# A nine-stage kernel whose stages meet once instead of twice, without GpSimd's Drain after three of them, and with one pair of down products moved forward

## The reference

```
h = layernorm(x)*(1+ca)+sa;  x = x + ga * L0_attn(h)   # causal softmax attention and a "geo" attention
h = layernorm(x)*(1+cb)+sb;  x = x + gb * L0_ffn(h)    # 32 routed experts of 64, top 4, and a shared expert
...
xe = zeros(E, C, D).at[eid, posc].add(...)             # at most 128 tokens an expert
h  = silu(xe @ W1) * (xe @ W3);  ye = h @ W2
yrows = ye[eid, posc] * gate;    out = sum over the 4 choices + silu(X@sw1.T)*(X@sw3.T)@sw2.T
...
h = layernorm(x)*(1+ca)+sa;  x = x + ga * L1_attn(h)   # short convolutions and a weighted delta rule, chunks of 64
h = layernorm(x)*(1+cb)+sb;  x = x + gb * L1_ffn(h)    # RMS norm, top 2 of 8 experts, hidden 352
```

## Time and profile before

| | us |
|---|---|
| median of 3 runs | 2004.95 |
| lowest and highest | 2000.4, 2006.43 |
| profiled execution, its own time | 2002.02 |
| its span, first to last instruction | 2000.1 |

### The profile page before, as it was taken

The page is one execution under the profiler, slowest core; times in us unless marked ns, Lnnn a source line. Parts: engine busy times, 40 slices in busy tenths (PEclk is TensorE's granted clock), DMA queues, the critical chain, the costliest instruction groups (busy, mean ns, idle before and its releaser), DMA issues. The chain is left out here.

```text
span 2000.1 us, 50931 instructions
## 1 busy us (share of the span) xinstructions
PE 1612.7 (81%) x17727; PEld 1252.1 (63%) x17727; DVE 1473.4 (74%) x4099; ACT 1185.8 (59%) x2762; POOL 1096.3 (55%) x1141
## 2 busy tenths in 40 slices
PE   5599999998788695698847777777789607999994
PEld 4478888887577442344325555555568607999993
DVE  8688888887499542699979999999667624555556
ACT  4566666665279721577828888887366404565551
POOL 3278888887000286233348888888437773444440
PEclk8799999999899798799969999999766658999998
DMA  4000000000501132521000000000401112222216
GB/s 120 18 3 3 4 4 4 4 3 3 219 28 41 42 45 35 147 63 43 11 0 1 1 2 1 1 1 1 185 23 48 52 60 62 66 64 65 64 51 257
DMA packets 84954, 92.34 MB, mean 46 GB/s; under 512 B 11696, under 2 KB 69296, under 8 KB 84000
## 3 DMA queue, kind: packets, MB, share of 16 engines
q1 hardware_dynamic: 67840, 62.66, 9.9%
q0 software_dynamic: 14560, 22.24, 4.3%
q10 hardware_dynamic: 2304, 4.20, 0.5%
HBM read 46.14 MB, written 42.91 MB: 45 GB/s over the span
## 5 line engine op out<-in xcount | busy, mean ns | idle before, releaser
L2275 POOL TENSOR_TENSOR delta_A<-delta_A,delta_sW 128x256 f32<-128x256 f32 x256 | 193.7, 757 | 79.1 <-ACT delta_sW L2122 53.0
L2045 PE MATMUL delta_u<-delta_m,tables_sb 128*128 128x256 f32 x512 | 166.7, 407 | 82.0 <-DVE delta_m L2195 82.0
L694 ACT ACTIVATE attn_p_att<-attn_score,attn_mx 128x32 f32<-128x32 f32 (+7 forms) x512 | 150.4, 409 | 134.7 <-DVE attn_mx L756 134.7
L2895 POOL DMA_INDIRECT choice_rows<-ffn_y,ffn_xg x135 | 129.7, 961 | 170.9 <-DVE ffn_y L3002 167.4
L2122 ACT ACTIVATE delta_sW<-delta_W,tables_sb 128x256 f32<-128x256 f32 x256 | 126.7, 506 | 79.9 <-DVE delta_W L2217 76.1
L2045 PEld LDWEIGHTS delta_u<-delta_m,tables_sb 128*128 128x128 f32 x512 | 87.1, 190 | 132.7 <-DVE delta_m L2195 126.0
L2041 PE MATMUL delta_u<-delta_v_own,tables_sb 128*128 128x256 f32 x512 | 153.8, 383 | 8.7 <-DVE xnT L2182 8.7
L2852 POOL DMA_INDIRECT rows<-mix_rows,mix_slot x128 | 125.5, 980 | 47.9 <-issue 38.6
L1324 POOL DMA_INDIRECT exp_rows<-rows,slot_token x32 | 33.1, 1033 | 190.4 <-SPq L142 180.9
L2217 DVE TENSOR_TENSOR delta_W<-delta_W,delta_u 128x128 f32<-128x128 f32 x512 | 133.1, 280 | 4.5
L2204 DVE TENSOR_TENSOR delta_u<-delta_u,delta_prod 128x256 f32<-128x256 f32 x256 | 109.8, 429 | 17.8 <-PE delta_u L2045 4.2
(11 more groups left out here) (396 smaller groups left out, 4691.4 us busy)
## 6 DMA issues: line engine op xcount, KB each, us to landing
ffn_xg<-rows SPq DMA_DIRECT2D x135, 66.0 KB, 1.8
acc<-route_zero SPq DMA_DIRECT2D x10, 832.0 KB
comb_rows<-choice_rows SPq DMA_DIRECT2D x32, 256.0 KB, 5.3
rows<-route_rows SPq DMA_DIRECT2D x8, 640.0 KB, 3.5
load_rows<-in_x SPq DMA_DIRECT2D x16, 256.0 KB, 3.8
bT<-acc SPq DMA_DIRECT2D x16, 256.0 KB, 4.1
qT<-acc SPq DMA_DIRECT2D x16, 256.0 KB, 4.7
x_kept<-xT SPq DMA_DIRECT2D x16, 256.0 KB, 2.1
```

Of the source, the lines that this page charges most:

```text
L694: last = nc.scalar.activation(p_att[:, gr, PAIR_OFF[n]:PAIR_OFF[n] + SLOT * (n + 1)], S[:, gr, c:c + SLOT * (n + 1)], ACT.Exp, bias=mx[:, ...
L2045: nc.tensor.matmul(corrections(h, pp % 2), g.t("same_head"), m1[:, h].rearrange("p t d b -> p (t d b)"), start=False, stop=True).then_inc( ...
L2275: nc.gpsimd.tensor_tensor(A[:, t % 8], A[:, (t - 1) % 8], sW[:, t % RING], ALU.add).then_inc(k.A, 1)
L2895: nc.gpsimd.indirect_dma_start(g.choice_rows, bass.IndirectOffsetOnAxis(xg[:, n % RING, D:D + 1].bitcast(U32), 0), y[:, n % RING, :], None ...
```

## The change

1. Leaving a scope no longer clears semaphores and no longer holds the second meeting. The scope's semaphores go onto a list, `Scope.retired`.
2. Opening the next scope's block clears what is on the list, on GpSimd, in front of its branch into that stage. Since the next stage takes its semaphores before that, it gets other numbers, and what is cleared one stage later can be two ranges instead of one. At the end of the program the last scope is cleared and one `all_engine_barrier()` is held.
3. The blocks of the experts, the mix and the FFN are closed without GpSimd's Drain. The other engines issue their Drain there, then signal and wait with semaphore instructions.
4. In the experts' round 0 TensorE makes the down products after `shared_down(0)` and in front of `turn(1)` and `shared_up(1)`, and VectorE makes `y` in front of `add_shared(0)`. Rounds 1 to 15 are as before.

```diff
--- before.py
+++ after.py
@@ -123,6 +123,8 @@
 class Scope(ExitStack):
 
 
+    retired = []
+
     def __init__(self, nc, name):
         super().__init__()
         self.nc, self.name, self.taken = nc, name, []
@@ -142,11 +144,12 @@
         super().__exit__(*exc)
         if exc[0] is None:
 
-            self.nc.clear_and_free_semaphores(self.taken)
-            self.nc.all_engine_barrier()
-
-    def block(self):
-        return self.enter_context(self.nc.Block())
+            Scope.retired.append(self.taken)
+
+    def block(self, drain=True):
+        while Scope.retired:
+            self.nc.clear_and_free_semaphores(Scope.retired.pop())
+        return self.enter_context(self.nc.Block(no_gpsimd_drain=not drain))
 
 
 RC = CH // SLOT
@@ -1315,7 +1318,7 @@
         gate_ps, val_ps, shared = s.ps("gate_ps"), s.ps("val_ps"), s.ps("shared")
         c = s.sems("sw_ready w13 w2 turned x_copied up gate hid down y up_s gate_s hid_s shared x_done added0 added1")
         gathered = [s.sems("gathered", n).gathered for n in range(LAST + 1)]
-        block = s.block()
+        block = s.block(drain=False)
         chunk = lambda i: bass.ds(i * CH, CH)
 
         @block.gpsimd
@@ -1386,10 +1389,13 @@
             for i in range(0, LAST + 1):
                 make_up(i)
                 shared_down(i)
+                if i == 0:
+                    make_down(i)
                 if i < LAST:
                     turn(i + 1)
                     shared_up(i + 1)
-                make_down(i)
+                if i > 0:
+                    make_down(i)
 
         @block.scalar
         def _(act):
@@ -1454,8 +1460,11 @@
             shared_hidden(0)
             for i in range(0, LAST + 1):
                 hidden(i)
+                if i == 0:
+                    output(i)
                 add_shared(i)
-                output(i)
+                if i > 0:
+                    output(i)
                 if i < LAST:
                     shared_hidden(i + 1)
 
@@ -3203,6 +3212,9 @@
         mix_phase(nc, dram, g)
         ffn_phase(nc, dram, g)
         combine_phase(nc, dram, g, out)
+        while Scope.retired:
+            nc.clear_and_free_semaphores(Scope.retired.pop())
+        nc.all_engine_barrier()
 
 
 def kernel(**inputs):
```

## The result

| | us |
|---|---|
| median of the changed kernel, 5 runs | 1981.78 |
| lowest and highest | 1979.2, 1984.25 |
| median before, then 5 runs | 2003.12 (2000.4 to 2006.43) |
| ratio to before, 95% interval | 0.9893 (0.9877 to 0.9908) |
| profiled execution, its own time | 1984.25 |

The change takes 21.3 us off.

A forecast was written before the change was run, and what follows sets the result against it. No engine fills any stage, so the time is nine stage lengths plus what lies between them. Meetings 6.0 - 0.1, Drains 9.8 - 0.1 and round 0 1.0 make 16.6 us: 2004.95 to 1988.4, said as 1988, range 1982 to 1996.

The forecast's parts named there:

- Second meetings, 6.0: At eight transitions between stages, the time from first to second release goes, together 6.0 us; the ninth, at the end, stays.
- Three Drains, 9.8: GpSimd's Drains after experts, mix and FFN (5.28, 1.44, 3.08 us) leave the transitions and are hidden in the next stages: 9.8.
- GpSimd now meets them as the Drain in front of the clear: The three Drains do not vanish but move to the next stage's start, covered there; cost 0.1 us at the projection.
- First gather, nothing lost: Experts' first gather is held until VectorE's cast of `w13` ends, so the whole 0.6 us is kept; otherwise 0.4 is lost.
- Round 0, 1.0: Experts' round 0: earlier down products and `y` free GpSimd's first addition; most returns as a wait before the third; gain 1.0 us.
- I take 0.2 for what is not given back: Delay of `turn(1)` and `shared_up(1)` by the early down products, not regained before `make_up(1)`: 0.2 us off 1.2.
- later rounds of `y` have 1.2 us of slack more each: In the experts, each `y` after round 1 has 1.2 us of slack more.
- Rivals 2 to 4: Drain's wait returns as later landings (1998.2, chance 0.05); code fetches exposed at transitions (1997.2, 0.06); fetches queue there (2014.8, 0.04).
- The sum: Whole kernel: 6.0 - 0.1 + 9.8 - 0.1 + 1.0 = 16.6 us gained.
- the median before is 2.9 us above the profiled execution, and the forecast for the median is 2004.95 - 16.6: Base of the whole-kernel forecast: median before 2004.95 us, profiled execution 2002.02; less 16.6 gives 1988.4, said as 1988.

The follow-up runs named there:

- plain Drain behind the release: Changed kernel with one plain GpSimd Drain added in front of each clear, at the start of the next stage; 2040.94 us in one run.
- the first comparison: First measurement of the changed kernel against the kernel before, five runs each: 1981.78 against 2003.12 us, ratio 0.9893.
- series 1: Later measurements of each part alone and the changed kernel again (1982.81 us, ratio 0.9914), beside 17 runs of before (median 2001.76).
- series 3: Later measurements beside 23 runs of before (2049.32 us): changed kernel a third time 2041.15, ratio 0.9943; with round 1 reordered too 2038.15, ratio 0.9944.

## Why the prediction was right and wrong, point by point

- **Second meetings, 6.0: right, perhaps more.** The change alone gives 9.4 (6.0 to 12.6). The stages that have only this term fell, in the means of three traces each, by 1.5 (attention), 0.3 (route) and 1.1 us (delta), where 0.7, 0.7 and 0.9 were forecast.
- **Three Drains, 9.8: the size right, the mechanism wrong.** Alone they give 11.6 (8.2 to 15.2). The step that failed is "GpSimd now meets them as the Drain in front of the clear": that Drain takes 0.1 us. Why the clear's Drain doesn't take the cost over is open. The error cost nothing in the sum, because the place where the prediction put the three Drains was covered anyway, as the plain Drain behind the release shows: the size came right without the mechanism.
- **First gather, nothing lost: right.** 2.33 us long against 2.3 forecast, ending 1.0 after the cast, and it moves with the cast. That a whole gather is left when the cast ends holds for this case (1.0 us) and not for the one that begins with the cast (0.1).
- **Round 0, 1.0: the place right, the size a little high.** The stage's length gives 0.5 to 0.9. The term that was mis-sized is "I take 0.2 for what is not given back". `y` of round 1 stands 22.3 us behind the first release, before 22.4, though the cast that it descends from gained 0.6: 0.5 was not given back. The queue order is not where it went: the up products of round 1 start 16.5 us behind the release, before 17.0. But they run at the lower clock and take 1.80 us, not 1.09, so they end 18.3 behind it, before 18.1. 1.2 - 0.5 is 0.7. Whether the new order keeps the clock low is not shown. It is back at full speed 15.9 us behind the release in the three traces of before, and 17.8 to 18.0 in the traces of the changed kernel and of round 0 only, which speaks for it. In three traces with round 1 changed too, where TensorE has the same work in the same order up to then, it is back at 14.8, 16.3 and 17.8. Of the new wait of 2.8 us 0.3 is the gap that every issue there has; the rest is 2.5 where 2.0 was forecast. In the changed kernel's traces no addition from the fourth to the 25th waits, as "later rounds of `y` have 1.2 us of slack more each" has it.
- **Rivals 2 to 4: refuted.** The projection's loads land as before (5.3 us behind their issue, before 5.2), and the FFN and the combine fell too. The first instruction of the projection comes 0.1 us behind the release, and the stages' first VectorE work 0.1 to 0.5 (but in the combine, where it waits for its loads): no code fetch is laid bare. The rule of the Trainium skill ("Runtime: NRT & Kernel Launch", section "Instruction fetch mechanics") is that a taken branch stalls when its target is outside the pages held. No such stall shows at these transitions; no trace shows whether the targets were outside.
- **The sum.** 14.6 of the 16.6 us lie outside the mix, and 15.6 were measured there. In the mix 2.0 were forecast; in the first comparison and series 1 the two traces with before's transitions have 233.7 and 230.7, the two of the change 231.8 and 227.8: 2.4 on average, no more than two executions of one kernel differ (4), and in series 3 the sign is the other.
- **What was wrong is the base and the spread.** The step "the median before is 2.9 us above the profiled execution, and the forecast for the median is 2004.95 - 16.6" took a median of three runs that 22 runs put at 2001.8. From there the same sum gives 1985.2, and the measured medians are 1981.8 and 1982.8. The miss of 6.2 us is so made of about 3 from the base and about 3 from the difference. (By the five runs of before in the first comparison alone, 2003.12, it is 1.8 from the base and 4.7 from the difference of 21.3.) The difference itself is 21.3, 17.2 and 11.7 us in three comparisons; 16.6 is within the last two intervals and 1.8 us under the first (18.4 to 24.6). Single traces of one kernel differ by some 3 us outside the mix, and by 4 in it within the first comparison and series 1. So whether 2 or 3 us of real gain are missing from the sum is open, and which term they would belong to as well. With the base at 2001.8 the same range would have begun near 1979 and held the time: the base is the step that put it outside. And a range that starts at 1982 was too near to its own forecast for such a spread.

## What to carry to other kernels

Price a transition by the gap from the last arrival to the next stage's first work, and look at each Drain in it: one on GpSimd behind indirect DMAs can cost microseconds when no work is left, and the Drain of a clear in its place almost nothing. Take the base from as many runs as can be had, because an error in it goes whole into the forecast. A wait that is removed inside a pipeline comes back a round or two later unless the chain that feeds the bounding engine moves in those rounds too.

## What was not expected of the hardware

- GpSimd's plain Drain as the first one after indirect DMAs: 5.28 us (after 64 of them), 1.44 (after 128) and 3.08 (after 135), equal to 0.02 us in every trace and with or without traffic. So it does not go by the number of DMAs alone. Its length is the same whether it begins 0.1 us behind the branch that follows GpSimd's last wait or 0.3, with all semaphores come, which speaks against a wait for data on their way. The clear's Drain in its place takes 0.1 us, and a plain one behind that and the clear 0.05. What it does was not settled.
- One stage of a kernel, the mix, took 228 to 234 us in some series and 277 to 291 in others, while the eight others together agree to some 3 us for each of the two kernels. By the numbers on record a chip and a length of the mix don't go together (chip 3 has both), and the cause is open.
- In one of the three traces with rounds 0 and 1 in the new order TensorE's clock fell behind a gap in its work: 0.56 and 0.59 from 708 to 712 us; in the 2 us from 704 TensorE had been busy for 0.87, in the next 2 for 1.88. That the gap made it fall is not shown.
